# The expert phase of a graph and mixture-of-experts layer: every accumulating scatter waits for the one ahead of it

## What is computed

```
xn = layernorm(x) * gamma + beta
top_vals, top_idx = top_k(xn @ Wr + br, 2)
w = softmax(top_vals)
for e in range(8):
    h = gelu(xn @ W1[e] + b1[e])
    y = y + (h @ W2[e] + b2[e]) * w_full[..., e, None]
out = x + y
```

## Time and profile before

| | us |
|---|---|
| three executions | 1593.35, 1601.96, 1606.03; median 1601.96 |
| the profiled execution, its own time | 1592.01 |
| span of its trace, from the first to the last instruction | 1590.2 |
| mean granted clock of TensorE over the span | 0.921 of full speed |
| first scatter of the expert phase starts at | 1193.45 |
| last scatter (the 105th) starts at | 1580.06 |

### The profile page before, as it was taken

One profiled execution on the slowest core, in us unless ns is written; L12 is line 12 of the kernel. 1 busy time (PEld: TensorE's weight loads), 2 busy tenths in 40 slices (PEclk: granted clock), 3 DMA queues, 4 the chain that ended last, 5 costly groups with the idle time before them and its releaser, 6 DMA issues. The chain is left out here.

```text
span 1590.2 us, 30753 instructions
## 1 busy us (share of the span) xinstructions
PE 1296.5 (82%) x8310; PEld 1136.1 (71%) x8311; DVE 991.7 (62%) x2925; ACT 536.6 (34%) x1414; POOL 826.6 (52%) x820
## 2 busy tenths in 40 slices
PE   1897477777778788888888887788569999999996
PEld 1785366666767677777776666666349999999996
DVE  3998466655656777766767637877854444444443
ACT  1665400011111222323332110033635555555553
POOL 2001566656665666666666651033016676666664
PEclk9999688889897999999999998899659999999998
DMA  6003423323334555666677780023864444444442
GB/s 200 12 0 111 137 80 87 90 80 90 84 103 137 150 152 171 174 173 178 192 222 233 239 241 28 1 94 106 263 121 67 68 67 73 67 70 71 71 67 36
DMA packets 138327, 183.06 MB, mean 115 GB/s; under 512 B 27232, under 2 KB 116014, under 8 KB 138100
## 3 DMA queue, kind: packets, MB, share of 16 engines
q0 software_dynamic: 44400, 92.92, 25.4%
q1 hardware_dynamic: 91844, 88.19, 18.5%
q10 hardware_dynamic: 1984, 0.81, 0.2%
HBM read 149.38 MB, written 33.41 MB: 115 GB/s over the span
## 5 line engine op out<-in xcount | busy, mean ns | idle before, releaser
L717 POOL DMA_INDIRECT RG<-table,srci x504 | 493.5, 979 | 284.7 <-issue 125.1
L734 PEld LDWEIGHTS ps<-S_t,RG 128*128 128x128 f32 x2016 | 285.5, 209 | 26.8 <-issue 11.3
L734 PE MATMUL ps<-S_t,RG 128*128 128x96 f32 x2016 | 286.6, 290 | 9.8 <-issue 6.7
L988 DVE TENSOR_TENSOR R<-R,ps 128x392 f32 x280 | 157.6, 563 | 178.0 <-remote 91.1
L756 PE MATMUL ps<-zrow,R 128*128 128x256 f32 x686 | 205.3, 405 | 21.1 <-DMA zrow<-table 10.3
L1978 POOL DMA_INDIRECT out<-R,S_t x105 | 166.7, 1588 | 98.5 <-DVE R L1948 58.9
L1861 PE MATMUL ps<-R,RG 128*128 128x128 f32 x1680 | 206.6, 277 | 0.0
L1871 PE MATMUL ps<-R 128*128 x840 | 198.5, 379 | 0.0
L1861 PEld LDWEIGHTS ps<-R,RG 128*128 128x128 f32 x1680 | 197.6, 193 | 0.3 <-issue 0.2
L1894 ACT ACTIVATE R<-ps,RG 128x128 f32<-128x128 f32 x420 | 119.7, 368 | 175.3 <-PE ps L1861 145.7
L1944 DVE TENSOR_TENSOR R<-ps,R 128x256 f32<-128x256 f32 x105 | 44.6, 425 | 200.5 <-PE ps L1871 196.6
(11 more groups left out here) (358 smaller groups left out, 1985.6 us busy)
## 6 DMA issues: line engine op xcount, KB each, us to landing
zrow<-table SPq DMA_DIRECT2D x336, 128.0 KB
RG<-table,srci POOLq DMA_INDIRECT x504
table<-RG SPq DMA_DIRECT2D x12, 512.0 KB, 2.9
out<-R SPq DMA_DIRECT2D x12, 512.0 KB, 3.2
ntable<-R SPq DMA_DIRECT2D x12, 512.0 KB
R<-in_x SPq DMA_DIRECT2D x6, 896.0 KB
R<-in_w SPq DMA_DIRECT2D x8, 514.0 KB, 8.0
slot<-in_x SPq DMA_DIRECT2D x32, 128.0 KB
```

The lines of the kernel that those rows point to most:

```text
L717: nc.gpsimd.indirect_dma_start(out=grows[:, s, :], out_offset=None, in_=table, in_offset=bass.IndirectOffsetOnAxis(ap=srci[:, ND + q, c:c ...
L734: last = nc.tensor.matmul(window(q % 2)[:, h, :], grows[:, s, h * P:(h + 1) * P], S_t[:, q % 2, c, :], start=c == 0, stop=c == GC - 1)
L988: nc.vector.tensor_tensor(win, win, psK[m % 2][:, 0:T * DW].rearrange("p (j w) -> p j w", w=DW), ALU.add).then_inc(cnt_ok, 1)
```

## The change

The condition that lets two scatters of one expert be in flight together goes. From t = 1 on, scatter t waits for the landing of scatter t-1, always; the wait for scatter t-2 goes, as it says nothing more. With it go SyncE's loop and `border`, the semaphore `turn_ok`, the two VectorE instructions of `border_waits`, and GpSimd's iota and copy for `late_f`.

```
-                nc.gpsimd.iota(late_i, pattern=[[16, (NTILE + 3) // 4], [0, 4]], base=0, channel_multiplier=0).then_inc(pl, 1)
                 nc.gpsimd.iota(code_i, pattern=[[P, 2 * T]], base=CODE0, channel_multiplier=1).then_inc(pl, 1)
-                pool.wait_ge(pl, 2)
-                nc.gpsimd.tensor_copy(late_f, late_i).then_inc(ready, 1)
+                pool.wait_ge(pl, 1)
                 nc.gpsimd.tensor_copy(code16, code_i).then_inc(ready, 1)
...
-                v.wait_ge(ready, 3)
+                v.wait_ge(ready, 2)
...
-                def border_waits():
-                    turn = slot[0:1, 0, 0:NTILE]
-                    ch.done(nc.vector.tensor_tensor(turn, eidf[:, 1:NTILE + 1], eidf[:, 0:NTILE], ALU.is_gt))
-                    ch.done(nc.vector.scalar_tensor_tensor(late, turn, 16.0, late_f[:, 0:NTILE], ALU.mult, ALU.add))
...
-                border_waits()
                 v.wait_ge(inv_ok, 1)
...
             def _(sp):
-                def border(t, s):
-
-                    n = nc.sync.value_load(late[0:1, bass.ds(t - 1, 1)], min_val=16, max_val=16 * (LOOPS + 1))
-                    sp.wait_ge(y_out[s], n)
-                    sp.sem_inc(turn_ok, 1)
-
-                with nc.sync.Fori(0, LOOPS - 1) as i:
-                    for u in range(4):
-                        border(i * 4 + (u + 5), u)
                 sp.wait_ge(b2_in, 16)
...
                 def scatter(t):
                     pool.wait_ge(y_ok, t + 1)
-                    if t >= 2:
-                        pool.wait_ge(y_out[(t - 2) % 4], 16 * ((t - 2) // 4 + 1))
-                    if 1 <= t < 5:
-                        pool.wait_ge(y_out[t - 1], 16)
-                    if t >= 5:
-                        pool.wait_ge(turn_ok, t - 4)
+                    if t >= 1:
+                        pool.wait_ge(y_out[(t - 1) % 4], 16 * ((t - 1) // 4 + 1))
                     nc.gpsimd.indirect_dma_start(
```

More of the change, by code:

```diff
@@ L1288, in build @@
         gat, sct, eid_i = ints[:, 0:NTILE], ints[:, NTILE:2 * NTILE], ints[0:1, 2 * NTILE:2 * NTILE + NSTEP]
-        late_i, late_f = ints[0:1, 430:430 + NTILE + 3], flat[0:1, 320:320 + NTILE + 3]
-        late = rt[0:1, 1240:1240 + NTILE].bitcast(i32)
         wpair = LA.rearrange("p t e -> p (t e)")[:, 0:2 * T].rearrange("p (t k) -> p t k", k=2)
@@ L1820, in build @@
             dv = semaphore(phase, "e_dve_order")
-            turn_ok = semaphore(phase, "e_border_passed")
             y_out = [semaphore(phase, f"e_y_stored{k}") for k in range(4)]
```

## The result

The changed kernel takes 1698.49 us (median of four executions, 1696.78 to 1700.58); the kernel before, beside it, 1600.55 (1593.35 to 1606.03). The ratio is 1.0618, with a 95% interval from 1.0586 to 1.0651: 98 us slower, where +93 and 1692 had been forecast.

The account below looks back on a forecast made before the run. TensorE bounded at 3.73 us per tile; scatter landings would. Steps of 434.0, 30.1, 4.6 and 11.1 make 479.8 against 386.6; +93.2 on the mean 1598.3 gives 1692 us, range 1677 to 1711 for 8 in 10.

Parts of the forecast that it names:

- The bound: Expert phase: each scatter's wait for the landing ahead bounds at 4.667 us per tile, replacing TensorE's 3.73; 87%.
- 93 full steps at 4.667: Expert phase, steps behind full tiles: priced from the old trace's first three strict steps, together 434.0 us.
- The seven partly padded steps at 4.3: Steps behind an expert's last, partly padded tile: between 3.93 and 4.67 us, middle 4.3, together 30.1.
- The three steps behind padding at 3.7: Last three steps, behind tiles with padding alone: 3.7 us each, together 11.1.
- The Trainium skill's figure: GpSimd's transfers: about 2.0 us plus bytes over 436 GB/s, 2.30 for 128 KB; set aside as adding 15 us.
- Nothing for what goes: Removed VectorE and GpSimd instructions and SyncE's loop: no gain, the relay below 0.1 us on each of seven steps.
- TensorE's cover: Gather through TensorE to ready rows: takes 17.6 us of 23.3, about 5.8 to spare, so landings still set the step.
- rival 3: Expert phase: TensorE, idle 0.93 of each 4.67, loses its clock; decides below mean 0.80, 1800 us at 0.64; 3%.
- hidden: Expert phase: the wait is hidden, time stays at 1602 us within 1%, steps at or under 3.73; 2%.
- half hidden: Steady part of the expert phase: steps come to 4.2 us, 43 less, 1649; 3%.
- a dearer step: Expert phase: steps of 4.9 us, as the gather's rows move beside the scatter's, 21 more, 1713; 5%.

Follow-up runs that it names:

- fixed borders: The changed kernel, but only the seven scatters that begin an expert wait for the scatter ahead, others for the one two ahead: 1463.55 us, ratio 1.0012.
- the wait alone: The kernel before with every tile marked as a border, so scatters wait through SyncE's relay, table and loop kept: 1573.53 us, ratio 1.0764.
- one strict step in three: The changed kernel, but only every third scatter and those that begin an expert wait for the scatter ahead: 1464.71 us, ratio 1.0016.
- half the matmuls: The kernel before with 8 of the 16 matmuls of `hidden` left out: 1555.54 us; the changed kernel with the same cut: 1697.68.
- scatters of 64 rows: The changed kernel with only the first 64 rows of each tile scattered, the others left out: 1636.39 us, ratio 1.0238.
- the two runs with the relay: The kernel before with every tile marked as a border, relay kept, run on two chips: 1573.53 us (ratio 1.0764) and 1702.28 (1.0652).

## Why the prediction was right

**The bound.** The step that carries it held: in place of TensorE's 3.73 a tile costs the strict step, which the first scatters of the old trace showed already. 1692 against 1698.49, +93 against +98, released by landings as foretold. That the wait is the cause and no other part is shown by the fixed borders (+1.2) and by the wait alone (+111, relay included). Two forecasts beside it were off: the first and the last scatter start at 1201 and 1688, not near 1193 and 1673, and TensorE is busy 85% and not 80%. Counted by its matmuls, a tile keeps it busy 3.98 us here and 3.73 before; the clock, 0.99, explains little of that, and the rest is open.

**The terms of the sum**, for the phase 479.8 forecast and 487.3 measured:
- 93 full steps at 4.667: the mean is 4.74, which makes 440.5 for 434.0. The three steps of the start were a small sample, 4.61 to 4.72; the upper bound of 4.72 that I drew from them is the later median, 4.71. Four steps of the 93 are longer for another reason, below, and make 2.6 of the 6.5; they were not foreseen.
- The seven partly padded steps at 4.3: they sum to 31.5 and not 30.1. Only two of the seven are short, 3.89 and 3.99, behind tiles with 5 and 13 rows, so that padding is no reason for a short step unless almost no row is left; the middle between shortest and longest was a poor estimate, and a list of all seven in the old trace would have given 30.9.
- The three steps behind padding at 3.7: 3.56, 3.52 and 3.53. The direction was right, the size 0.5 too much in sum.

The Trainium skill's figure ("DMA: Bandwidth & Descriptors", section "Anatomy of one DMA — SWDGE (gpsimd) path"), which I had set aside for the rows, comes out at the median if 2.30 is put behind the descriptors: 1.59, 2.30 and 0.83 for the release make 4.72. Part of that is luck. In the trace the landing comes 3.82 behind the start, 2.23 behind the descriptors, and the next start 0.88 behind the landing. The section also counts the setup into its fixed part, and from the start of the instruction 2.30 would be far below 3.82. And the working was wrong where I set it aside: a step of 4.72 adds 0.05 to my 4.667, so 93 steps add 5 us and not 15.

**Nothing for what goes.** Held: no difference with fixed borders.

**TensorE's cover.** Its conclusion held, its size was off: I had 5.8 us to spare. The second instruction of `weighted` for tile 21 ended at 1290.97 (the 22nd run of line 1928), scatter 21 started at 1299.19: less the 0.83 of release, 7.4 ahead, and about 8 in most of the phase. That VectorE's `weighted` would wait for landings was wrong: the rows are one to two tiles ahead and not three, because the gathers pace them, so that `weighted` never comes to a buffer that is still in flight, and line 1924 waits for TensorE, 162.7 us.

**The clock, rival 3.** It dipped once in the phase. The stretches around it, and VectorE's second instructions of tiles 15, 16 and 17 with the scatter of tile 16:

```profile
1262.00:1266.00 4.00, 2.21 (x11) 2.17 (x12) 1.68 (x6) 0.16 (x1) 2.58 (x2) 0.72 0.43 51
1266.00:1270.00 4.00, 4.00 (x25) 3.75 (x25) 0.39 (x1) 2.09 (x5) 2.58 (x2) 0.85 0.33 53
1270.00:1274.00 4.00, 4.00 (x31) 3.75 (x30) 1.99 (x9) 2.09 (x5) 1.94 (x2) 1.00 0.24 45
```
```profile
1262.38 0.35 DVE L1928 TENSOR_SCALAR R<-R 128x256 f32<-128x256 f32 x1
1270.07 0.35 DVE L1928 TENSOR_SCALAR R<-R 128x256 f32<-128x256 f32 x1
1273.71 0.35 DVE L1928 TENSOR_SCALAR R<-R 128x256 f32<-128x256 f32 x1
```
```profile
1276.50 1.59 POOL L1954 DMA_INDIRECT out<-R,S_t  x1 [1.86 <-DMA out<-R,S_t]
```

Tile 16 came 7.69 behind tile 15 and not 4.7, and its scatter still waited for the landing: the cover was eaten to 5.3 and nothing was lost. With TensorE busy 85%, the mean over 300 us was 0.99, far above the 0.80 from which it decides. The rule of the Trainium skill ("TensorE: Matmul & The Clock Gate", section "A second HAM failure mode: psum-queue depth-cycling"), that short idle times between groups make the clock go up and down, hardly shows in this stretch.

**Rivals 1, 2 and 4** (hidden, half hidden, a dearer step): no step behind a full tile is under 4.57, and only 5 of the 93 reach the dearer one of 4.9.

## What to carry to other kernels

A wait for a DMA's landing ahead of each transfer puts issue, landing and release in a row, in place of the issuing engine's floor (here 4.72 for 3.19). Look whether the trace of the old kernel has a few such steps already, as here at its start and at its borders: they price the new one. What it costs is the sum over a round against the engine that bounds, not the number of waits: with one strict step in three nothing was lost. And an order that only data at borders need is worth its relay here: 0.05 us for a step against 0.98.

## What was not expected

GpSimd has rare late starts that don't come from the landing. Steps 36 and 72 of the strict kernel are 5.65 and 5.58, and in the second profile of the same kernel 5.68 and 5.55. The rows around the first:

```profile
1369.72 1.59 POOL L1954 DMA_INDIRECT out<-R,S_t  x1 [1.79 <-DMA out<-R,S_t]
...
1375.37 1.59 POOL L1954 DMA_INDIRECT out<-R,S_t  x1 [2.77 <-DVE R L1928]
```

The releaser that is named can't be the cause, as the rows had been ready for 9 us. Nor is the landing late: by its last semaphore event in the trace it came 3.87 behind the start at 1369.72, as usual, and the next scatter started 1.78 behind it in place of 0.88. The kernel before has the same late start; with half the matmuls, where GpSimd never stands idle there, it is absent:

```profile
1332.62 1.59 POOL L1978 DMA_INDIRECT out<-R,S_t  x1 [1.50 <-issue]
```
```profile
1325.89 1.59 POOL L1978 DMA_INDIRECT out<-R,S_t  x1 [0.30 <-issue]
```

Both rows are scatter 37; in the first its rows had been ready for 1.74 us, in place of 0.83. All runs with strict scatters of 128 rows have the late starts at 37 and 73, with the relay too. With scatters of 64 rows the single such step is another, 60 (5.48). So it may go with the number of descriptors or transfers rather than with time or program; what it is stays open, no run was made for it.

Three more steps (10, 42 and 74) are some 0.3 longer: there the next start comes 1.17 to 1.20 behind the landing. These stand at the same places with scatters of 64 rows, but not in the two runs with the relay. So they go with the program and are something else. Step 42 is one of the seven behind a partly padded tile.

One chip ran the kernel before in 1462 us and the others in 1596 to 1601, and the expert phase was equal to 0.2 us where it was compared. In the stretch from 200 to 560 TensorE is granted 0.97 of full speed there (run with fixed borders) against 0.88:

```profile
200.00:560.00 360.00, 315.89 (x2107) 286.00 (x2108) 278.35 (x911) 73.28 (x245) 274.33 (x282) 0.97 0.48 137
```

More gets done in the same stretch, 2107 matmuls against 1716. Whether the clock is the cause or follows is open.
